# Keeping five of sixteen weight pieces of a feed-forward layer in SBUF in a fused RWKV block

## The chip, the cores and the metric

The kernel runs on one core of a Trainium2 chip. The metric is the device time of one launch in microseconds. The core has five engines that run their own instruction streams and wait for each other through semaphores: TensorE (PE), VectorE (DVE), ScalarE (ACT), GpSimd (POOL) and SyncE (SP), whose queue issues nearly all transfers here. Sixteen DMA engines move the data.

## The reference

x has shape (4, 2048, 512), fp32, 8192 tokens. The attention half works on a layer norm of x; the feed-forward half on a layer norm of what comes out.

```python
xx = jnp.pad(x, ((0, 0), (1, 0), (0, 0)))[:, :T] - x
r, k, v, g = (x + xx * maa_m) @ Wm.T ...        # 512 x 512 each, 32 heads of 16
# in chunks of 64 tokens, with a state per head:
att = rc @ kc * w_mat
yc = att @ vc + rc @ state * wb
state = ws * state + kc * wk @ vc
x = x + (group_norm(y) * silu(g)) @ Wo.T
# feed-forward, 512 -> 2048 -> 512
D = gelu(layernorm(x).astype(float16) @ W0.T + bias0).astype(float16)
x = x + (D @ W1.T + bias1).astype(float16)
```

## The kernel before

The tokens go through in nb = 32 blocks of 256 (two tiles of 128). A step n does the attention of block n, the rest of the attention (group norm, gate, output projection Wo) of block n-1, the feed-forward of block n-2 up to the first half of its down projection, and the second half of the down projection of block n-3. The order of the work on each engine is written out by hand (pe_step, dve_steady, act_steady, sp_steady); every dependence is a semaphore with a constant count. Steps 3 to 31 are alike ("steady"); there x and y are transposed by DMA (x_words, y_words) and not on TensorE.

The feed-forward weights are 16 pieces of 0.5 MB: pieces 0 to 7 for the up projection (W0), 8 to 15 for the down projection (W1). Each piece is [128, 2048] fp16: a scaled high part and a low part that the fp16 rounding of the high part left. Steps 0 and 1 prepare them ("PREPARED_AT"): load raw fp32 (sp_raw), square sums on ScalarE (act_piece_square, L382), a scaled high half (act_high), its transpose by DMA (sp_high), the transposed low half through TensorE (pe_prepare L836, act_prepare L851), and two stores of both halves to the DRAM tensor wd (sp_prepared). place_of says where piece j is prepared: slots of ring for j < 5, then hT, then a half of x1.

From step 2 on all 16 pieces are streamed once per block from wd through ring, which has RING = 5 slots. Transfer number `use` goes into slot use % 5 and is issued by sp_weights as soon as the piece five uses before has been consumed (s_up or s_dn). TensorE waits for s_w of the slot in pe_up (16 matmuls of 256 columns per piece) and pe_down (8 of 512 columns per piece).

In a steady step TensorE does, in this order: K0, down 4, K1, down 5, R0, down 6, R1, down 7, V0, up 0, V1, up 1, up 2, up 3, scores, kv, G0, up 4, scores, up 5, G1, up 6, att·v, up 7, from_state, scores, Wo 0, down 0, kv, scores, down 1, Wo 1, down 2, att·v, from_state, down 3. The scores, kv, att·v and from_state parts are many short matmuls of 64 rows. K, R, V and G are projections at L879 and L911, Wo is L1040, up is L1068, down is L1132, scores L941, from_state L982, kv L1012.

SP's queue in a steady step (sp_steady) issues: weights for `use` 0 to 2, the transpose for the feed-forward input (sp_fx), kx, x_words, weights 3, rx, the kN transpose (L2027), weights 4, y_words (L2043), weights 5, vbd (L2051), weights 6, vbd, out, weights 7 to 9, x1's load of x (L2077), xa's load of x (L2080), weights 10 to 15. An SP instruction that waits holds up all that stand behind it.

Of the kernel before, what the change touches and what calls it, by code (L numbers as in the profile page):

```python
# [21 lines left out]
NH = HID // P  # L22
UNITS = 16
RING = 5
LN_EPS = 1e-5
GN_EPS = 1e-5 * 144
KS = 2.0 ** 10
# [65 lines left out]
def program(nc, ctx, a, consts, x, out, wd, nb):  # L93
# [26 lines left out]
    f_scl = sb("f_scl", [P, PIECES + 1])  # L120
    f_sum = sb("f_sum", [P, 2 * PIECES])
    f_most = sb("f_most", [P, 1])
    ring = sb("ring", [P, RING, 2, 2 * C], F16)
    hT = sb("hT", [P, NH, BT], F16)
    x1 = sb("x1", [P, 2, NT, C])
# [219 lines left out]

    def place_of(j):
# [7 lines left out]
    def raw_piece(j):  # L356
        return place_of(j).bitcast(F32)

    def parts_of(j):

        return place_of(j)[:, 0:2 * C], place_of(j)[:, 2 * C:4 * C]

    def sp_raw(eng, n, j):
        if n == 0:
            source = W0[2 * P * j:2 * P * (j + 1), :]
        else:
            eng.wait_ge(s_stash[j], 32)
            source = W1[:, 2 * P * j:2 * P * (j + 1)]
        if n == 0:
            eng.dma_start(raw_piece(j).rearrange("p (b c) -> p b c", b=2),  # L370
                          source.rearrange("(b p) c -> p b c", p=P)).then_inc(s_raw[j], 16)
        else:
            for i in range(2):
                eng.dma_start(raw_piece(j)[:, C * i:C * i + C].rearrange("p (b c) -> p b c", b=G),
                              source[:, P * i:P * i + P].rearrange("(b p) c -> p b c", p=P)).then_inc(s_raw[j], 16)

    def act_piece_square(eng, n, j, squares):
        q = PIECES * n + j
        eng.wait_ge(s_raw[j], 48 if n else 16)
        if due(q):  # L380
            eng.wait_ge(s_psq, q)
        eng.activation(squares, raw_piece(j), ACT.Square, accum_out=f_sum[:, q:q + 1]).then_inc(s_psq, 1)  # L382

    def dve_power(eng, k, done, at, most, root, scale):

# [415 lines left out]
    def act_high(eng, q):  # L801

        k = min(q, PIECES)
        eng.wait_ge(s_pscl, POW2_PER * (q // PIECES) + POW2_PER - 1)
        if q <= PIECES:
            if k >= DIAGONALS:
                eng.wait_ge(s_ptr, k - DIAGONALS + 1)
            eng.activation(diagonals[k % DIAGONALS], ident[:, :], ACT.Identity, scale=f_scl[:, k:k + 1]).then_inc(s_diag, 1)
        eng.wait_ge(s_raw[q % PIECES], 48 if q >= PIECES else 16)
        j = q % PIECES  # L810
        if j % 3 == 2:
            eng.wait_ge(s_vwl, NT * (q // PIECES + 1))
# [4 lines left out]
        eng.activation(high(q), raw_piece(q % PIECES), ACT.Identity, scale=f_scl[:, k:k + 1]).then_inc(s_phi, 1)  # L817

    def pe_prepare(eng, n, place):

        q = piece(n, place)
        if q is None:
            return
        k = min(q, PIECES)
        eng.wait_ge(s_raw[q % PIECES], 48 if q >= PIECES else 16)
        eng.wait_ge(s_minus, 1)
        eng.wait_ge(s_diag, k + 1)
        eng.wait_ge(s_phi, q + 1)
        if due(q):
            eng.wait_ge(s_plo, q)  # L830
        else:
            eng.wait_ge(s_wlo, 10)
        for i in range(2):
            for b in range(G):
                at = C * i + P * b
                eng.matmul(F[:, i, rows(b)], raw_piece(q % PIECES)[:, at:at + P], diagonals[k % DIAGONALS],  # L836
                           start=(b == 0), stop=False)
            for b in range(G):
                at = C * i + P * b
                mm = eng.matmul(F[:, i, rows(b)], high(q)[:, at:at + P], minus_one[:, :],  # L840
                                start=False, stop=(b == G - 1))
        mm.then_inc(s_ptr, 1)

    def act_prepare(eng, n, place):

        q = piece(n, place)
        if q is None:
            return
        eng.wait_ge(s_ptr, q + 1)
        eng.wait_ge(s_psq, q + 1)  # L850
        eng.activation(parts_of(q % PIECES)[1], F[:, :, :].rearrange("p k c -> p (k c)"), ACT.Copy).then_inc(s_plo, 1)  # L851
        if q == 1:
            act_high(eng, 2)
        if 0 < q < PIECES - 2 or PIECES <= q < 2 * PIECES - 2:
            act_high(eng, q + 2)

    def sp_high(eng, q):

        eng.wait_ge(s_ptr, q + 1)
        eng.wait_ge(s_psq, q + 1)  # L860
        eng.dma_start_transpose(parts_of(q % PIECES)[0].rearrange("p (k c) -> p k c", c=P), high(q)).then_inc(
            s_phT[q % PIECES], 16)

    def sp_prepared(eng, q):
        j = q % PIECES
        eng.wait_ge(s_plo, q + 1)
        eng.wait_ge(s_phT[j], 16 * (q // PIECES + 1))
        for a in range(2):
            eng.dma_start(wd[q].rearrange("p (k a c) -> p a k c", k=2, a=2)[:, a],
                          parts_of(j)[a].rearrange("p (k c) -> p k c", k=2)).then_inc(s_stash[j], 16)  # L870

# [176 lines left out]
    def pe_up(eng, n, j):  # L1048

        f = n - 2  # L1050
        use = UNITS * f + j
        eng.wait_ge(s_w[use % RING], 16 * (use // RING + 1))
        if j == 0:
            eng.wait_ge(s_fx, 16 * (f + 1))
        if j >= 2:
# [9 lines left out]
        for i in range(2):  # L1065
            for a in range(2):
                for kk in range(G):
                    mm = eng.matmul(up_place(f, j)[:, i * BT:(i + 1) * BT],  # L1068
                                    ring[:, use % RING, i, a * C + kk * P:a * C + (kk + 1) * P], xT[:, :, kk, :],
                                    start=(kk == 0 and a == 0), stop=(kk == G - 1 and a == 1))  # L1070
        mm.then_inc(s_up, 1)

# [7 lines left out]
    def pe_last_down(eng):  # L1080
# [2 lines left out]
        eng.wait_ge(s_h, NH * nb)  # L1083
        for t, at, width, count in LAST_PARTS:
            for j in range(4, 8):
                use = UNITS * f + 8 + j
# [10 lines left out]
    def pe_down_of_last(eng, j):  # L1097

        f = nb - 1
        use = UNITS * f + 8 + j  # L1100
# [15 lines left out]
    def pe_down(eng, f, j):  # L1116
        if f == nb - 1:
            pe_down_of_last(eng, j)
            return
        use = UNITS * f + 8 + j  # L1120
# [874 lines left out]

    def sp_weights(eng, use):

        if use >= UNITS * nb:
            return
        gone = use - RING  # L2000
        if gone >= 0:
            f, i = gone // UNITS, gone % UNITS
            if i < 8:
                eng.wait_ge(s_up, 8 * f + i + 1)
            else:
                eng.wait_ge(s_dn, 8 * f + i - 7)
        eng.dma_start(ring[:, use % RING, :, :], wd[use % UNITS].rearrange("p (k e) -> p k e", k=2)).then_inc(
            s_w[use % RING], 16)

    def sp_stack(eng, dst, src, which, landed):  # L2010
# [41 lines left out]

    def sp_steady(eng, n, ahead):

        use = UNITS * (n - 2) - 4 + RING - 1
        p = n - 1
        for i in range(3):
            sp_weights(eng, use + i)
# [18 lines left out]
        eng.dma_start(x1[:, p % 2, :, :], x_rows(x, p)).then_inc(s_xr[p % 2], 16)  # L2077
        if n + 2 < nb:
            eng.wait_ge(s_xw, 2 * (n + 2 - BY_DMA))
            eng.dma_start(xa[:, :, :], x_rows(x, n + 2)).then_inc(s_xa, 16)  # L2080
        for i in range(10, 16):
            sp_weights(eng, use + i)

    def sp_step(eng, n):
        att_n, tail, ff, ahead, late = in_step(n)
        if tail and y_by_dma(n - 1):
            sp_steady(eng, n, ahead)
            return
        use = UNITS * (n - 2) - 4 + RING - 1
        if n > nb and ff:  # L2090
            sp_fx(eng, n - 2)
        if late:
# [29 lines left out]
        if ff:  # L2122
            sp_weights(eng, use + 5)
# [5 lines left out]
        if ff:  # L2129
            sp_weights(eng, use + 6)  # L2130
        if tail:
            p = n - 1
            if due(p - 1):
# [4 lines left out]
        if ff:  # L2138
            sp_weights(eng, use + 7)
        if n + 2 < nb:  # L2140
            if n + 1 < BY_DMA:
                eng.wait_ge(s_X, NT * (n + 2))
# [12 lines left out]
            sp_raw(eng, 1, PIECES - 1)  # L2155
        if n == 1:
            for j in range(PIECES):
                eng.wait_ge(s_stash[j], 64)
                if j < RING:
                    sp_weights(eng, j)  # L2160
        if ff:
            for i in range(8, 16):
                sp_weights(eng, use + i)

    steps = range(nb + 3)
# [83 lines left out]
```

## Time and profile before

| | us |
|---|---|
| median of 3 runs | 2085.12 (2084.56 to 2085.14) |
| the profiled execution, its own time | 2075.69 |
| its span, first to last instruction | 2073.9 |
| TensorE busy | 2002.3 |
| VectorE busy | 1738.2 |
| ScalarE busy | 1293.5 |
| DMA, main queue | 77.2% of 16 engines' span |

The profile shows one execution. Its times are counted from the first instruction. "Idle before" a group is time in which its engine did nothing, with what released it; "issue" stands where the profile shows nothing that the engine waited for. SPq is the time an instruction of SP's queue took to issue. The granted clock is a share of full speed; 1.00 is 2.4 GHz and 0.50 is 1.2 GHz.

### The profile page before, as it was taken

To read this page: it belongs to the slowest core of one execution; us is meant where nothing else is said; L and a number is where in the kernel's file an instruction comes from. 1 tells how busy PE (TensorE), PEld (TensorE's weight loads), DVE (VectorE), ACT (ScalarE), POOL (GpSimd) and SP (SyncE) were. 2 spreads that over 40 slices of the span, in tenths; PEclk is the share of its full clock that TensorE was granted. 3 is DMA by queue.
4 is the path that set the end of the run, shared out by engine and by line. 5 is a ranking of instruction groups with operands and counts; after the bars stand their busy time and mean duration, and the time that the engine had idled before them with its cause. 6 is when DMAs were issued, how large, how long until landed. Compare 5 with 4: busy or idle time off the path is not lost.

```text
span 2073.9 us, 64752 instructions
## 1 busy us (share of the span) xinstructions
PE 2002.3 (97%) x27206; PEld 1423.9 (69%) x27206; DVE 1738.2 (84%) x3687; ACT 1293.5 (62%) x2081; POOL 317.5 (15%) x329
## 2 busy tenths in 40 slices
PE   5889999999999999999999999999999999999999
PEld 5777667667666767766766776676776667667666
DVE  7778889888888988888988888898888888888761
ACT  7876565676566666655657765666765656666452
POOL 1111111111111111111111111111111111111110
PEclk8999999999999999999999999999999999999999
DMA  6977677888777788777778877778887877887777
GB/s 214 220 199 237 177 236 216 248 239 233 200 233 220 236 241 241 213 226 227 230 231 245 248 203 225 234 215 247 250 231 202 231 220 230 250 238 203 216 249 250
DMA packets 428979, 471.97 MB, mean 228 GB/s; under 512 B 259600, under 2 KB 309392, under 8 KB 428688
## 3 DMA queue, kind: packets, MB, share of 16 engines
q1 hardware_dynamic: 427056, 467.64, 77.2%
q8 instruction: 216, 3.54, 0.7%
q14 instruction: 75, 0.61, 0.1%
q10 hardware_dynamic: 1632, 0.18, 0.1%
HBM read 316.21 MB, written 25.17 MB: 165 GB/s over the span
## 4 chain that ended last, share of the span: by engine, by line
PE 81%; DMA 4%; SPq 4%; DVE 3%; ACT 3%; issue 3%; POOL 0%; ACTq 0%; DVEq 0%
PE F L1132 20%; PE F L1068 17%; PE B L879 10%; PE B L1040 8%; PE sc L879 7%; PE YT L911 6%; PE YT L879 3%; PE YT L963 2%; DMA y<-ygT 2%; PE sc L941 2%; PE YT L982 2%; DMA ring<-w_dram 1%; SPq L2027 1%; PE YT L1012 1%; PE F L836 1%
## 5 line engine op out<-in xcount | busy, mean ns | idle before, releaser
L1132 PE MATMUL F<-ring,hT 128*128 128x512 f16 x1984 | 467.5, 379 | 0.0
L1068 PE MATMUL F<-xT,ring 128*128 128x256 f16 x3840 | 449.3, 273 | 5.1 <-ACT hT L1768 3.7
L1068 PEld LDWEIGHTS F<-xT,ring 128*128 128x128 f16 x3840 | 369.8, 98 | 64.9 <-issue 8.0
L1132 PEld LDWEIGHTS F<-ring,hT 128*128 128x128 f16 x1984 | 189.1, 98 | 197.9 <-issue 0.5
L879 PE MATMUL B<-mix,WT 128*128 128x256 f16 x2304 | 267.5, 273 | 0.4 <-DVE gT L1372 0.3
L1768 ACT ACTIVATE hT<-F,b,f_rho 128x256 f16<-128x256 f32 x480 | 243.5, 560 | 37.9 <-PE F L1068 37.9
L879 PEld LDWEIGHTS B<-mix,WT 128*128 128x128 f16 x2304 | 222.6, 98 | 33.8 <-DVE gT L1372 0.6
L276 DVE SCALAR_TENSOR_TENSOR mixf<-dx,maa,xnT 128x256 f32<-128x256 f32 x512 | 238.6, 526 | 0.1
L1725 ACT ACTIVATE Shl<-S 128x256 f16<-128x256 f32 x128 | 53.1, 415 | 263.7 <-PE YT L982 148.6
L1971 POOL TENSOR_TENSOR Shl<-S,Shl 128x256 f16<-128x256 f32 x128 | 89.2, 697 | 734.7 <-ACT Shl L1725 734.7
L1719 ACT ACTIVATE att<-att 128x512 f16<-128x512 f32 x256 | 147.5, 624 | 68.3 <-DVE att L1333 68.3
L336 DVE TENSOR_TENSOR mix<-mixf,mix 128x1024 f16<-128x1024 f32 x128 | 184.0, 1438 | 2.9 <-ACT mix L332 1.8
L1040 PE MATMUL B<-WT,yg 128*128 128x512 f16 x768 | 180.1, 385 | 4.2 <-issue 4.2
L879 PE MATMUL sc<-mix,WT 128*128 128x256 f16 x1536 | 179.3, 274 | 4.7 <-issue 2.6
L1339 DVE TENSOR_TENSOR att<-att 128x512 f16<-128x512 f32 x256 | 166.7, 692 | 16.4 <-ACT att L1719 16.3
L911 PE MATMUL YT<-WT,mix 128*128 128x512 f16 x768 | 176.0, 379 | 0.6 <-DVE f_rho L389 0.3
L1333 DVE TENSOR_TENSOR att<-sc,wmask 128x512 f32<-128x512 f32 x256 | 164.2, 683 | 13.5 <-PE sc L941 13.1
L879 PEld LDWEIGHTS sc<-mix,WT 128*128 128x128 f16 x1536 | 150.6, 98 | 35.7 <-issue 5.2
L1976 POOL TENSOR_TENSOR x<-e,x 128x512 f32<-128x512 f16 x62 | 70.7, 1161 | 577.7 <-DVE e L1412 577.7
L332 ACT ACTIVATE mix<-mixf 128x1024 f16<-128x1024 f32 x128 | 134.6, 1051 | 4.6 <-DVE mixf L276 4.2
L1040 PEld LDWEIGHTS B<-WT,yg 128*128 128x128 f16 x768 | 72.9, 99 | 91.5 <-issue 9.1
L1654 ACT ACTIVATE kT<-sc 128x512 f16<-128x512 f32 x64 | 38.1, 596 | 155.0 <-PE sc L879 155.0
(196 smaller groups left out, 2997.6 us busy)
## 6 DMA issues: line engine op xcount, KB each, us to landing
ring<-w_dram SPq DMA_DIRECT2D x512, 512.0 KB, 4.6
kx<-kT SPq DMA_DIRECT2D x96, 256.0 KB, 3.8
rx<-rT SPq DMA_DIRECT2D x96, 256.0 KB, 4.4
xa<-in_L_attn_x SPq DMA_DIRECT2D x32, 512.0 KB, 7.6
vbd<-vN SPq DMA_DIRECT2D x256, 64.0 KB, 3.1
x<-in_L_attn_x SPq DMA_DIRECT2D x32, 512.0 KB, 6.1
out<-x SPq DMA_DIRECT2D x31, 512.0 KB, 3.8
w_dram<-ring SPq DMA_DIRECT2D x20, 256.0 KB, 3.8
```

The lines of the kernel that those rows point to most:

```text
L276: last = eng.scalar_tensor_tensor(out=mixf[:, m % 2, g, :], in0=dx[:, g, :], scalar=maa[:, m, g:g + 1], in1=xnT[:, g, 1:BT + 1], op0=ALU.m ...
L332: eng.activation(mix[:, m % 2, 0, :, :], mixf[:, m % 2, :, :], ACT.Copy).then_inc(s_mh, 1)
L336: eng.tensor_tensor(mix[:, m % 2, 1, :, :], mixf[:, m % 2, :, :], mix[:, m % 2, 0, :, :], ALU.subtract).then_inc(s_ml, 1)
L879: mm = eng.matmul(out[:, gg * BT:(gg + 1) * BT], WT[:, w, a, kk, rows(g)], mix[:, m % 2, b, kk, :], start=(i == 0 and kk == 0), stop=(i == ...
L911: mm = eng.matmul(Y[:, t, :], mix[:, 0, a, kk, rows(t)], WT[:, V_, b, kk, :], start=(i == 0 and kk == 0), stop=(i == 2 and kk == G - 1))
L1040: mm = eng.matmul(B[:, :], yg[:, a, kk, rows(t)], WT[:, O_, b, kk, :], start=(i == 0 and kk == 0), stop=(i == 2 and kk == G - 1))
L1068: mm = eng.matmul(up_place(f, j)[:, i * BT:(i + 1) * BT], ring[:, use % RING, i, a * C + kk * P:a * C + (kk + 1) * P], xT[:, :, kk, :], st ...
L1132: mm = eng.matmul(F[:, t, :], hT[:, k, rows(t)], ring[:, use % RING, i, a * C:(a + 1) * C], start=(k == 0 and a == 0), stop=(k == NH - 1 a ...
L1333: eng.tensor_tensor(att32[:, x, :], sc[:, x, :], wmask[:, 8 * x:8 * x + 8, :].rearrange("p q i -> p (q i)"), ALU.mult).then_inc(s_am, 1)
L1339: eng.tensor_tensor(att[:, c % 2, 1, C * x:C * x + C], att32[:, x, :], att[:, c % 2, 0, C * x:C * x + C], ALU.subtract).then_inc(s_al, 1)
L1719: eng.activation(att[:, c % 2, 0, C * x:C * x + C], att32[:, x, :], ACT.Copy).then_inc(s_ah, 1)
L1768: eng.activation(hT[:, k, :], up_place(f, j)[:, i * BT:(i + 1) * BT], ACT.Gelu, bias=b0[:, k:k + 1], scale=f_rho[:, j:j + 1]).then_inc(s_h, 1)
```

## The change

A tensor kept of [128, 5, 2, 1024] fp16 (20 KB per partition) is added. Up pieces 0 to 4 are prepared in it and stay there for the whole run; their stores to wd fall away. TensorE reads them from kept in pe_up, in the layout in which they were prepared (all high parts, then all low parts). The ring serves the other eleven pieces (up 5 to 7, down 0 to 7), so a step issues 11 weight transfers instead of 16. In the queue of a steady step, the weight issues around vbd and the three behind out fall away; xa's load moves ahead of x1's load, and between them stands weights 5, which waits for up 5. A scratch area that the program sets aside for DMA is made smaller (1024 bytes).

```diff
+KEPT = 5
+STREAMED = UNITS - KEPT
...
+    kept = sb("kept", [P, KEPT, 2, 2 * C], F16)
...
+    def place_of(q):
+        j = q % PIECES
+        if q < KEPT:
+            return kept[:, q, :, :].rearrange("p a e -> p (a e)")
         if j < RING:
             return ring[:, j, :, :].rearrange("p k e -> p (k e)")
...
     def sp_raw(eng, n, j):
         if n == 0:
             source = W0[2 * P * j:2 * P * (j + 1), :]
         else:
-            eng.wait_ge(s_stash[j], 32)
+            if j >= KEPT:
+                eng.wait_ge(s_stash[j], 32)
...
     def sp_prepared(eng, q):
         j = q % PIECES
+        if q < KEPT:
+            return
...
     def pe_up(eng, n, j):
-        use = UNITS * f + j
-        eng.wait_ge(s_w[use % RING], 16 * (use // RING + 1))
+        use = STREAMED * f + j - KEPT
+        if j >= KEPT:
+            eng.wait_ge(s_w[use % RING], 16 * (use // RING + 1))
+        elif f == 0:
+            eng.wait_ge(s_phT[j], 16)
...
+                    w = kept[:, j, a, i * C+at:i * C + at + P] if j < KEPT else ring[:, use % RING, i, a * C + at:a * C + at + P]
...
     def sp_weights(eng, use):
-        if use >= UNITS * nb:
+        if use >= STREAMED * nb:
             return
         gone = use - RING
         if gone >= 0:
-            f, i = gone // UNITS, gone % UNITS
+            f, i = gone // STREAMED, gone % STREAMED + KEPT
...
     def sp_steady(eng, n, ahead):
-        use = UNITS * (n - 2) - 4 + RING - 1
+        use = STREAMED * (n - 2)
...
         sp_weights(eng, use + 4)
         sp_y_words(eng, p)
-        sp_weights(eng, use + 5)
         sp_vbd(eng, n, 0)
-        sp_weights(eng, use + 6)
         sp_vbd(eng, n, 1)
         eng.wait_ge(s_o, NT * (n - 2))
         eng.dma_start(x_rows(out, n - 3), x1[:, (n - 3) % 2, :, :]).then_inc(s_st, 16)
-        for i in range(7, 10):
-            sp_weights(eng, use + i)
-        eng.wait_ge(s_st, 16 * (p - 1))
-        eng.dma_start(x1[:, p % 2, :, :], x_rows(x, p)).then_inc(s_xr[p % 2], 16)
         if n + 2 < nb:
             eng.wait_ge(s_xw, 2 * (n + 2 - BY_DMA))
             eng.dma_start(xa[:, :, :], x_rows(x, n + 2)).then_inc(s_xa, 16)
-        for i in range(10, 16):
+        sp_weights(eng, use + 5)
+        eng.wait_ge(s_st, 16 * (p - 1))
+        eng.dma_start(x1[:, p % 2, :, :], x_rows(x, p)).then_inc(s_xr[p % 2], 16)
+        for i in range(6, STREAMED):
             sp_weights(eng, use + i)
```

## Rows read from the trace of the kernel before

**Rows 1.** The page: busy times, DMA queues, one DMA issue with its landing.

```profile
PE 2002.3 (97%) x27206; PEld 1423.9 (69%) x27206; DVE 1738.2 (84%) x3687; ACT 1293.5 (62%) x2081; POOL 317.5 (15%) x329
...
q1 hardware_dynamic: 427056, 467.64, 77.2%
q8 instruction: 216, 3.54, 0.7%
...
x<-in_L_attn_x SPq DMA_DIRECT2D x32, 512.0 KB, 6.1
```

**Rows 2.** The chain that ended last, over the span: start us, us, what.

```profile
209.30 4.38 PE B L1040 x12
...
250.13 5.24 PE F L1068 x48
...
271.05 2.70 PE B L1040 x12
...
310.19 5.24 PE F L1068 x48
...
1861.78 4.24 PE B L1040 x12
...
1962.52 5.24 PE F L1068 x48
```

**Rows 3.** Waits of TensorE from 250 to 2000: us in total, times, longest.

```profile
PE sc L941 <- issue: 12.3, 11, 2.5
PE YT L982 <- issue: 4.4, 4, 1.3
PE B L1040 <- issue: 4.2, 3, 2.3
PE F L1068 <- ACT hT L1768: 2.9, 6, 0.7
```

**Rows 4.** Timeline of TensorE, two of the gaps.

```profile
1249.65 0.32 PE L941 MATMUL sc<-rx,kx 64*64 64x64 f16 x15 [1.48 <-issue]
...
1682.36 0.28 PE L941 MATMUL sc<-rx,kx 64*64 64x64 f16 x9 [0.83 <-issue]
```

**Rows 5.** Windows: us, busy of each engine (instructions), PEclk, DMA share, GB/s.

```profile
1861.40:1864.90 3.50, 3.44 (x15) 1.38 (x16) 3.09 (x5) 1.69 (x3) 0.00 (x0) 0.51 0.82 325
1244.29:1248.29 4.00, 3.88 (x148) 3.19 (x145) 3.36 (x6) 3.56 (x8) 0.97 (x1) 1.00 1.03 392
1248.29:1252.29 4.00, 2.64 (x27) 1.30 (x28) 3.93 (x7) 2.45 (x6) 0.67 (x1) 1.00 1.04 416
...
1256.29:1264.29 8.00, 8.00 (x142) 4.34 (x141) 4.91 (x13) 2.00 (x4) 1.28 (x2) 1.00 0.48 169
```

**Rows 6.** Timeline of SP's queue in an undisturbed step: start us, us.

```profile
1162.64 4.18 SPq L2027 DMA_TRANSPOSE kN<-kT  x1
...
1179.06 2.54 SPq L2007 DMA_DIRECT2D ring<-w_dram  x3
1182.62 0.38 SPq L2077 DMA_DIRECT2D x<-in_L_attn_x  x1
```

**Rows 7.** Timeline of SP's queue in step 1.

```profile
115.18 2.78 SPq L2027 DMA_TRANSPOSE kN<-kT  x1
```

**Rows 8.** Waits from 84 to 125: us in total, times, longest.

```profile
PE B L343 <- ACT xa L284: 1.9, 1, 1.9
...
ACT ygT L382 <- DMA x<-in_L_ffn_W: 0.7, 1, 0.7
```

**Rows 9.** Waits of TensorE from 2000 to the end.

```profile
PE YT L1068 <- DMA ring<-w_dram: 1.0, 1, 1.0
```

**Rows 10.** Timeline of TensorE in the step of rows 6.

```profile
1178.17 1.92 PE L1068 MATMUL F<-xT,ring 128*128 128x256 f16 x16
...
1188.16 2.76 PE L1040 MATMUL B<-WT,yg 128*128 128x512 f16 x12
...
1195.12 2.75 PE L1040 MATMUL B<-WT,yg 128*128 128x512 f16 x12
```

More of the change, by code:

```diff
@@ L344, in pe_X @@
         tr.then_inc(s_X, 1)
-    def place_of(j):
+    def place_of(q):
+        j = q % PIECES
+        if q < KEPT:
+            return kept[:, q, :, :].rearrange("p a e -> p (a e)")
         if j < RING:
@@ L354, in place_of, with raw_piece, parts_of, stashed @@
         return x1[:, 1, :, :].rearrange("p t c -> p (t c)").bitcast(F16)
[L356 to L361, printed above, removed]
+    def raw_piece(q):
+        return place_of(q).bitcast(F32)
+    def parts_of(q):
+        return place_of(q)[:, 0:2 * C], place_of(q)[:, 2 * C:4 * C]
+    def stashed(j):
+        return 32 if j < KEPT else 64
     def sp_raw(eng, n, j):
@@ L366, in sp_raw @@
         else:
-            eng.wait_ge(s_stash[j], 32)
+            if j >= KEPT:
+                eng.wait_ge(s_stash[j], 32)
             source = W1[:, 2 * P * j:2 * P * (j + 1)]
         if n == 0:
-            eng.dma_start(raw_piece(j).rearrange("p (b c) -> p b c", b=2),
+            eng.dma_start(raw_piece(PIECES * n + j).rearrange("p (b c) -> p b c", b=2),
                           source.rearrange("(b p) c -> p b c", p=P)).then_inc(s_raw[j], 16)
@@ L373, in sp_raw @@
             for i in range(2):
-                eng.dma_start(raw_piece(j)[:, C * i:C * i + C].rearrange("p (b c) -> p b c", b=G),
+                eng.dma_start(raw_piece(PIECES * n + j)[:, C * i:C * i + C].rearrange("p (b c) -> p b c", b=G),
                               source[:, P * i:P * i + P].rearrange("(b p) c -> p b c", p=P)).then_inc(s_raw[j], 16)
@@ L381, in act_piece_square @@
             eng.wait_ge(s_psq, q)
-        eng.activation(squares, raw_piece(j), ACT.Square, accum_out=f_sum[:, q:q + 1]).then_inc(s_psq, 1)
+        eng.activation(squares, raw_piece(q), ACT.Square, accum_out=f_sum[:, q:q + 1]).then_inc(s_psq, 1)
     def dve_power(eng, k, done, at, most, root, scale):
@@ L816, in act_high @@
             eng.wait_ge(s_phT[(6, 7, 5)[j]], 16)
-        eng.activation(high(q), raw_piece(q % PIECES), ACT.Identity, scale=f_scl[:, k:k + 1]).then_inc(s_phi, 1)
+        eng.activation(high(q), raw_piece(q), ACT.Identity, scale=f_scl[:, k:k + 1]).then_inc(s_phi, 1)
     def pe_prepare(eng, n, place):
@@ L835, in pe_prepare @@
                 at = C * i + P * b
-                eng.matmul(F[:, i, rows(b)], raw_piece(q % PIECES)[:, at:at + P], diagonals[k % DIAGONALS],
+                eng.matmul(F[:, i, rows(b)], raw_piece(q)[:, at:at + P], diagonals[k % DIAGONALS],
                            start=(b == 0), stop=False)
@@ L850, in act_prepare @@
         eng.wait_ge(s_psq, q + 1)
-        eng.activation(parts_of(q % PIECES)[1], F[:, :, :].rearrange("p k c -> p (k c)"), ACT.Copy).then_inc(s_plo, 1)
+        eng.activation(parts_of(q)[1], F[:, :, :].rearrange("p k c -> p (k c)"), ACT.Copy).then_inc(s_plo, 1)
         if q == 1:
@@ L860, in sp_high @@
         eng.wait_ge(s_psq, q + 1)
-        eng.dma_start_transpose(parts_of(q % PIECES)[0].rearrange("p (k c) -> p k c", c=P), high(q)).then_inc(
+        eng.dma_start_transpose(parts_of(q)[0].rearrange("p (k c) -> p k c", c=P), high(q)).then_inc(
             s_phT[q % PIECES], 16)
@@ L869, in sp_prepared @@
             eng.dma_start(wd[q].rearrange("p (k a c) -> p a k c", k=2, a=2)[:, a],
-                          parts_of(j)[a].rearrange("p (k c) -> p k c", k=2)).then_inc(s_stash[j], 16)
+                          parts_of(q)[a].rearrange("p (k c) -> p k c", k=2)).then_inc(s_stash[j], 16)
     def pe_project_T(eng, out, w, n, m, half):
@@ L1067, in pe_up @@
                 for kk in range(G):
-                    mm = eng.matmul(up_place(f, j)[:, i * BT:(i + 1) * BT],
-                                    ring[:, use % RING, i, a * C + kk * P:a * C + (kk + 1) * P], xT[:, :, kk, :],
+                    at = kk * P
+                    w = kept[:, j, a, i * C + at:i * C + at + P] if j < KEPT else ring[:, use % RING, i, a * C + at:a * C + at + P]
+                    mm = eng.matmul(up_place(f, j)[:, i * BT:(i + 1) * BT], w, xT[:, :, kk, :],
                                     start=(kk == 0 and a == 0), stop=(kk == G - 1 and a == 1))
@@ L1085, in pe_last_down @@
             for j in range(4, 8):
-                use = UNITS * f + 8 + j
+                use = STREAMED * f + 8 - KEPT + j
                 if t == 0:
@@ L1099, in pe_down_of_last @@
         f = nb - 1
-        use = UNITS * f + 8 + j
+        use = STREAMED * f + 8 - KEPT + j
         eng.wait_ge(s_w[use % RING], 16 * (use // RING + 1))
@@ L1119, in pe_down @@
             return
-        use = UNITS * f + 8 + j
+        use = STREAMED * f + 8 - KEPT + j
         eng.wait_ge(s_w[use % RING], 16 * (use // RING + 1))
@@ L2006, in sp_weights @@
                 eng.wait_ge(s_dn, 8 * f + i - 7)
-        eng.dma_start(ring[:, use % RING, :, :], wd[use % UNITS].rearrange("p (k e) -> p k e", k=2)).then_inc(
+        eng.dma_start(ring[:, use % RING, :, :], wd[KEPT + use % STREAMED].rearrange("p (k e) -> p k e", k=2)).then_inc(
             s_w[use % RING], 16)
@@ L2088, in sp_step @@
             return
-        use = UNITS * (n - 2) - 4 + RING - 1
+        use = STREAMED * (n - 2)
         if n > nb and ff:
@@ L2121, in sp_step @@
                               x1[:, (n - 3) % 2, t, at:at + width]).then_inc(s_st, 16)
-        if ff:
-            sp_weights(eng, use + 5)
         if att_n:
@@ L2128, in sp_step @@
             sp_prepared(eng, PIECES * n)
-        if ff:
-            sp_weights(eng, use + 6)
         if tail:
@@ L2137, in sp_step @@
             eng.dma_start(x1[:, p % 2, :, :], x_rows(x, p)).then_inc(s_xr[p % 2], 16)
-        if ff:
-            sp_weights(eng, use + 7)
         if n + 2 < nb:
@@ L2157, in sp_step @@
             for j in range(PIECES):
-                eng.wait_ge(s_stash[j], 64)
+                eng.wait_ge(s_stash[j], stashed(j))
                 if j < RING:
@@ L2161, in sp_step @@
         if ff:
-            for i in range(8, 16):
+            for i in range(5, STREAMED):
                 sp_weights(eng, use + i)
@@ L2231 @@
     from concourse.bass_utils import run_bass_kernel_spmd
-    nc = bacc.Bacc("TRN2", target_bir_lowering=False, num_devices=1)
+    nc = bacc.Bacc("TRN2", target_bir_lowering=False, num_devices=1, dynamic_dma_scratch_size=1024)
     arrays, aps, consts = {}, {}, {}
```

## The prediction, made before the changed kernel was run

> **What bounds the kernel now.** I read the page's busy shares first: TensorE is busy 97% of the span, VectorE 84%, ScalarE 62%, and the 16 DMA engines 77% [rows 1]. So only a little time can come back at all, and it has to come back on TensorE. I then measured what a step costs when nothing disturbs it. The same matmul group of the up projection starts at 250.13 and at 310.19: 60.06 us. From 250.13 to 1962.52 there are 28 steps, so a mean step is 61.16 us [rows 2]. The steady part therefore holds 28 x 1.10 = 30.8 us above its floor; the head holds some idle time more and the tail very little.
>
> The waits of TensorE between 250 and 2000 say what the excess is [rows 3]: 18 gaps, 12.3 + 4.4 + 4.2 = 20.9 us, in which the engine waited for nothing that the profile shows ("issue"), and 2.9 us for ScalarE's GELU. Not one microsecond is put down to a weight transfer. A kernel that looks as if it had a stream of 0.5 MB weights to get rid of is not waiting for weights.
>
> Where do the 18 gaps lie? I went through the timeline of TensorE. 14 of them, all of those above 0.9 us, lie in the short matmuls (64x64) behind up piece 7 of a step or in the first output projection right after; one of 1.48 us is shown. The other four, 0.83 us and less, come in the short matmuls behind down piece 0 [rows 4]. In the two windows that hold the gap of 1.48 us the DMA engines' share is 1.03 and 1.04. In the 8 us from 1256.29, with more short matmuls (x142 in all), the share is 0.48 and TensorE has no gap [rows 5]. The page has a queue that explains such gaps: "q8 instruction", 216 packets, 3.54 MB [rows 1]. TensorE runs 27,206 matmuls and as many weight loads; 3.54 MB over 54,412 is 65 B each, so q8 is TensorE's own program, some 250 instructions to a packet. That is my inference: short matmuls use up instructions faster than the next packet comes, and the packet travels over the same DMA engines as everything else.
>
> **The change part by part.** *Transfers.* Each step issues 11 weight transfers instead of 16. The five that go from the SP queue of a step are one ahead of each of the two vbd groups and the three at 1179.06 [rows 6]; they are released by up 0 to up 4. What is issued between 1178 and 1192 today is out, three weights, x, xa and three more weights (for up 5, 6, 7): nine transfers of 0.5 MB. At the 416 GB/s of the full window [rows 5] one takes 1.26 us, nine 11.3 us of 14: full, as the share says. After the change the same stretch has out, xa, x and three weights, six of them, 7.6 us; out and xa come 1 to 2 us earlier, since every removed issue ahead of them held SP (0.85 us each in the group of three). The share there should fall from 1.0 to about 0.5 to 0.6.
>
> *What this is worth in the 18 gaps.* The trace shows no packet's latency, so I bound it: nothing, if the time from request to use doesn't depend on the load, and all 20.9 us, if it does strongly. The nearest row is another operation that goes through the same engines: the kN transpose holds SP for 4.18 us in a loaded step and for 2.78 us in step 1, where fewer transfers are in flight [rows 6, 7], 1.4 us less. Gaps of 1.16 us mean that lose 1.4 us each would nearly vanish. Since the load halves and doesn't go away, I take two thirds: 14 us.
>
> The Trainium skill speaks against this ("Runtime: NRT & Kernel Launch", Instruction fetch mechanics): TensorE has a FIFO for 2048 instructions, refilled in blocks of 256, and crossing a block is "mostly hidden". The block agrees with 3.54 MB in 216 packets; "hidden" doesn't agree with the 20.9 us of issue gaps, unless these have another cause. By the rule the term would be 0 instead of 14 us, and the whole sum 8 us instead of 22.
>
> *What follows a gap.* Of the 30.8 us, about 20 are the issue gaps and 2.9 the GELU's; some 7.8 us are left. 1.5 us of that is a stretch right after the longest gap, in which the granted clock is 0.51, the lower of the two levels (1.2 GHz), and twelve matmuls take 4.24 us instead of 2.70 [rows 2, 5]. The rest are slivers around the gaps. They should go with their cause: I take 4 us, bounds 0 and 7.8.
>
> *The head.* Ten stores of 256 KB to DRAM go (pieces 0 to 4, two each), and the second half's loads of pieces 0 to 4 no longer wait for them. SP is the late one there: ScalarE waits 0.7 us for the last load of the second half, and TensorE, behind ScalarE, 1.9 us for the normalised xa [rows 8]. Of these about 1 us should go. At 209 us a gap is followed by twelve matmuls in 4.38 us instead of 2.70 [rows 2]; a part of gap and slow clock I count too, 2 us. That makes 3 us for the head; the bounds are 0 and 6 (1.9, 1.7 for the clock, and a gap of at most 2.5).
>
> *The tail.* Here a weight does stop TensorE, once, for 1.0 us at an up piece [rows 9]. Five of each block's up pieces need no load any more, so the ring runs further ahead. I take 1.3 us with the slivers beside it, bounds 0 and 2.
>
> *Costed at nothing.* Reading kept instead of ring costs TensorE the same matmul. Five waits per step are taken from it. The steady steps' 2.9 us of waits for the GELU come from the chain kx, x_words, rx, kN, y_words in SP's queue; all five weight issues ahead of y_words stay (same slots, same releases), so I take 0, bound 2.9. The other order: x1's load now stands behind the weights that wait for up 5. Up 5 ends at 1180.09 and x is issued at 1182.62 today [rows 6, 10]; it will come no later. xa moves ahead and is needed only in the next step. Weights 6 to 10 wait for up 6 and later, as their counterparts do today, and each is used over 10 us later.
>
> *Sum.* 14 + 4 + 3 + 1.3 = 22.3 us of the profiled execution's 2075.7 us (span 2073.9), which gives 2053.4 us. The shown median, 2085.1 us, is 9.4 us above that execution, and the trace can't say why. I take the same 22 us from it: 2063 us.
>
> **The rivals.** (a) *The gaps don't depend on the DMA load.* Then the tail's 1.3 us, the 1 us of the late load and some of the GELU waits remain: about 3.5 us, 2081.6 us, inside what counts as no change. For it: the gaps share the place of the shortest matmuls as well as that of the fullest DMA, and a single packet needs little bandwidth. Against: the second group of short matmuls has none. The Trainium skill's page "DMA: Bandwidth & Descriptors" (Queues, rings and completion order) has each DMA engine take turns between queues packet by packet, by which a full weight queue would delay a packet of the program hardly at all; no row shows the order, and by that rule this case holds.
>
> (b) *The gaps go entirely,* with the slivers, the clock and the GELU waits: 20.9 + 7.8 + 6 + 2 + 2.9 = 39.6 us, 2045.5 us. For it: the removed transfers stand right ahead of the gaps. Against: w for up 6 and up 7 still land in the middle of that stretch.
>
> (c) *Slower: the load of x comes late.* Place: the residual add behind the first output projection (L1303), which reads x1; the second projection waits for it. x is issued at 1182.62, lands 6.1 us later at 1188.7, the projection ends at 1190.9, and the second starts at 1195.1 [rows 1, 6, 10]. With 0.7 us for the add, the load may come 5.6 us later than now before TensorE stands. Each microsecond beyond is paid in 29 steps; if it came 6 us later, 0.4 x 29 = 12 us, 2075 us with the other gains, and at 7 us late 1.4 x 29 = 41 us, 2104 us. Against: the only new thing ahead of it is the wait for up 5, 2.5 us before its issue now.
>
> (d) *The stream shifts.* Five instructions fewer a step put the packet boundaries elsewhere. The boundaries already wander over the step (gaps come in only some steps), so I expect the same mean; if the shift were unlucky, a third more, 7 us, would come against a gain of 8: about 2084 us.
>
> **How the numbers follow.** Forecast 0.62; (a) 0.20; (b) 0.07; (c) 0.04; (d) 0.07. The forecast's own range is 2052 to 2075 us (gap term 7 to 20 us, slivers 1 to 7, head and tail 2 to 6). 0.2% of 2085 us, about 4 us, is what a measurement of this kernel can tell. The range 2050 to 2084 us takes in (a) and leaves out most of (b), (c) and half of (d). Faster: all of the forecast and (b), a quarter of (a), together 0.74. Same: the rest of (a) and half of (d), 0.18. Slower: (c) and half of (d), 0.08.
>
> **What would show it.** The DMA share over the span falls from 77% to about 67% (160 transfers of 1.26 us are 202 us, a tenth of the span), and in the 8 us behind up 6 of a step from 1.0 to about 0.6. "Issue" in TensorE's waits between 250 and 2000 falls from 20.9 to about 7 us and the mean step from 61.16 to below 60.6, the undisturbed step staying at 60.06. The tail shows no wait for ring. The GELU waits stay near 3 us. The prediction is wrong if the share falls and the issue gaps stay (a), or if L1303 waits for DMA (c).

## The result and the profile after

Five pieces kept took 31 us off. The changed kernel has a median of 2053.7 us (2050.8 to 2055.1, 4 runs) against 2084.8 us (2078.8 to 2085.1, 4 runs) for the kernel before; the ratio is 0.9855, 95% interval 0.9834 to 0.9877. Timed twice more it came to 0.9834 (0.9809 to 0.9859) and 0.9855 (0.984 to 0.987). The forecast was 2063 us, range 2050 to 2084: right in sign and mechanism, and 22 us where 31 were measured.

The page of the changed kernel, lines that answer to [rows 1]:

```profile
PE 1999.8 (98%) x27206; PEld 1424.3 (70%) x27206; DVE 1738.7 (85%) x3687; ACT 1293.0 (63%) x2081; POOL 317.5 (15%) x329
...
q1 hardware_dynamic: 401296, 381.12, 68.1%
q8 instruction: 215, 3.52, 0.7%
...
x<-in_L_attn_x SPq DMA_DIRECT2D x32, 512.0 KB, 5.0
```

TensorE does the same work (2.5 us less of busy time), the data queue carries 86.5 MB less and its share falls from 77.2% to 68.1%, as forecast (about 67%). q8, read in the prediction as TensorE's own program, has 215 packets instead of 216: if program delivery improved, it isn't because there is less of it. (With the five waits a step put back, e1 below, it is 216 again.)

The chain that ended last, same points as [rows 2]:

```profile
250.53 5.24 PE F L1086 x48
...
310.65 5.24 PE F L1086 x48
...
1940.54 5.24 PE F L1086 x48
```

The span falls by 24.9 us (2073.9 to 2049.0), and the three rows divide it. The head up to the first row is 0.4 us longer. The 28 steps between first and last row take 1690.0 instead of 1712.4 us, 22.4 less: 60.36 us a step instead of 61.16, over a floor of 60.1 that has not moved (250.53 to 310.65). The tail behind the last row is 108.5 instead of 111.4 us, 2.9 less.

Waits of TensorE in the steady part (248 to 1975 us), against [rows 3]:

```profile
PE F L1086 <- ACT hT L1785: 4.1, 8, 0.7
PE YT L995 <- issue: 0.5, 1, 0.5
PE F L1149 <- issue: 0.5, 1, 0.5
```

The issue gaps fell from 20.9 us in 18 places to 1.0 us in two (3.5 us in five places and 3.4 us in four in two more executions of the changed kernel). One of the 18, 1.1 us, lay behind 1962.52 and so counts for the tail; within the 28 steps it is 19.9 against 1.0 us, 18.9 less. The waits for the GELU went from 2.9 to 4.1 us. That makes 17.7 of the 22.4 us; the other 4.7 are what the prediction called slivers (idle pieces beside the gaps) and the slow clock behind them.

What the DMA engines do around the short matmuls has to be read at one offset in the step. The offset is counted from the start of the step's first value projection (V, L911 before, L924 after, 12 matmuls of 128x512). The two windows of full share in [rows 5] lie 24 to 28 and 28 to 32 us behind such a start (1220.29), around the short matmuls where most of the gaps lay. The same offsets in one step of the changed kernel (columns as in rows 5):

```profile
1172.47:1176.47 4.00, 4.00 (x163) 3.35 (x161) 2.80 (x6) 3.02 (x7) 0.47 (x1) 1.00 0.52 177
1176.47:1180.47 4.00, 4.00 (x27) 1.87 (x20) 3.93 (x7) 2.45 (x6) 0.67 (x1) 1.00 0.46 135
```

The share there was 1.03 and 1.04; now it is 0.52 and 0.46, while TensorE is busy for all of the 4 us of each window. Over all 29 steady steps the two windows have a mean share of 1.01 and 0.99 in the kernel before and of 0.67 and 0.42 in the changed one. The engines are no longer full, though far from idle.

### The profile page after: what moved, and what is told of

The parts are those of the page before. It is cut to its first block, busy times and chain, and to the rows that moved or that the text cites. A ratio compares the mean times of both kernels' runs of the same rounds, so it can differ in the third digit from the quotient of the medians.

```text
span 2049.0 us, 64453 instructions
## 1 busy us (share of the span) xinstructions
PE 1999.8 (98%) x27206; PEld 1424.3 (70%) x27206; DVE 1738.7 (85%) x3687; ACT 1293.0 (63%) x2081; POOL 317.5 (15%) x329
## 3 DMA queue, kind: packets, MB, share of 16 engines
q1 hardware_dynamic: 401296, 381.12, 68.1%
## 4 chain that ended last, share of the span: by engine, by line
PE 81%; SPq 4%; DVE 4%; ACT 4%; DMA 3%; issue 2%; POOL 0%; ACTq 0%; DVEq 0%
PE F L1149 19%; PE F L1086 16%; PE B L892 9%; PE B L1053 8%; PE sc L892 7%; PE YT L924 6%; PE YT L892 3%; DMA y<-ygT 3%; PE YT L976 3%; SPq L2044 2%; PE sc L954 2%; PE YT L995 2%; PE YT L1086 1%; PE F L847 1%; PE YT L1025 1%
## 5 line engine op out<-in xcount | busy, mean ns | idle before, releaser
L1086 PE MATMUL F<-xT,kept 128*128 128x256 f16 x2400 | 276.8, 273 | 2.0 <-issue 1.2
L1086 PEld LDWEIGHTS F<-xT,kept 128*128 128x128 f16 x2400 | 234.6, 98 | 42.1 <-issue 2.6
L924 PE MATMUL YT<-WT,mix 128*128 128x512 f16 x768 | 178.6, 383 | 1.3 <-DVE mix L339 0.9
L1086 PE MATMUL F<-xT,ring 128*128 128x256 f16 x1440 | 172.5, 273 | 4.1 <-ACT hT L1785 4.1
L1086 PEld LDWEIGHTS F<-xT,ring 128*128 128x128 f16 x1440 | 135.3, 98 | 23.3 <-issue 6.4
```

Of the source, the lines that this page charges most:

```text
L924: mm = eng.matmul(Y[:, t, :], mix[:, 0, a, kk, rows(t)], WT[:, V_, b, kk, :], start=(i == 0 and kk == 0), stop=(i == 2 and kk == G - 1))
L1086: mm = eng.matmul(up_place(f, j)[:, i * BT:(i + 1) * BT], w, xT[:, :, kk, :], start=(kk == 0 and a == 0), stop=(kk == G - 1 and a == 1))
```

## The experiments

The result leaves open whether the bytes, the place of the transfers, the order in the queue, the removed waits or the shifted instruction stream did it. Each ratio is to the kernel before on the same chip: 2081.1 us beside e1 to e4, 2083.8 us beside e5 to e7, 2081.7 us beside e8 and the last comparison. "Steady issue gaps" are TensorE's, summed over its waits from about 248 to 1975 us; the kernel before has 19.9 us of them.

**e1_waits_back: the stream.** The changed kernel with the five TensorE waits of a block put back, in each block, on a semaphore that has long been reached:

```
-        elif f == 0:
+        else:
             eng.wait_ge(s_phT[j], 16)
```

> The changed kernel, with one thing put back: in every block TensorE waits once more at each of up 0 to up 4, on a semaphore that is long past its value, so that its instruction stream is as long as in the kernel before, while the eleven transfers stay. Theory 1 (the issue gaps come from the DMA load ahead of them): no difference to the changed kernel, about 2051 to 2055 us, issue gaps between 250 and 1975 of 1 to 3 us. Rival (the shorter stream moved the packet boundaries of TensorE's program off the short matmuls): the gaps come back, 15 us or more of issue, 2070 us or more.

Measured: 2049.2 us, ratio 0.9859 (0.9835 to 0.9883), steady issue gaps 1.2 us. The gain stays, so neither the removed waits nor the shift of the instruction stream made it.

**e2_scratch_only: the SBUF that made room.** The kernel before with nothing but the smaller descriptor scratch that the change also sets:

```
-    nc = bacc.Bacc("TRN2", target_bir_lowering=False, num_devices=1)
+    nc = bacc.Bacc("TRN2", target_bir_lowering=False, num_devices=1, dynamic_dma_scratch_size=1024)
```

> The kernel before with the smaller scratch area for DMA and nothing else. Theory 1: nothing changes, a ratio of 1.000 within 0.2%, issue gaps near 21 us. Rival (the scratch size itself is part of the gain): a ratio below 0.996.

Measured: 2082.6 us, ratio 1.0019 (1.0005 to 1.0033), steady issue gaps 23.7 us. It gives nothing. It also serves as a second look at the kernel before: its profiled execution (2082.3 us) lies at the median of the kernel before, where the one of [rows 1] (2075.7 us) lies 9 us under it.

**e3_again_same_place: the bytes back, where they were.** The changed kernel, in which the five kept pieces are stored to DRAM in the head and read again into kept in every step: one ahead of each vbd group and three behind out, the places of the five transfers that the change removed. The part of the edit in SP's queue for a steady step:

```
+        sp_again(eng, n - 2, 0)
         sp_vbd(eng, n, 0)
+        sp_again(eng, n - 2, 1)
         sp_vbd(eng, n, 1)
         eng.wait_ge(s_o, NT * (n - 2))
         eng.dma_start(x_rows(out, n - 3), x1[:, (n - 3) % 2, :, :]).then_inc(s_st, 16)
+        for j in range(2, KEPT):
+            sp_again(eng, n - 2, j)
```

> The changed kernel, but the five kept pieces are stored to DRAM after all and loaded again into kept once per block, each as soon as its up piece is done, at the places in SP's queue where the five transfers stood before (one ahead of each vbd group, three behind out). TensorE's loads of its program and its matmuls are as in the kernel before, the transfers are sixteen again. Theory 1: the issue gaps come back, 15 to 21 us between 250 and 2000, and the time goes to 2072 to 2085 us. Rival (kept as such or the shorter stream or the order of xa and x was what helped): it stays within 5 us of the changed kernel, 2050 to 2058 us.

**e4_again_late: the same bytes, later.** As e3, but all five reads stand last in the step, behind the weights that wait for down 2:

```
         for i in range(6, STREAMED):
             sp_weights(eng, use + i)
+        for j in range(KEPT):
+            sp_again(eng, n - 2, j)
```

> The same sixteen transfers per block as in the run that loads kept again at the old place, but the five are issued at the end of the step, behind the weights that wait for down 2, where the DMA engines are half idle. Theory 1 (what counts is the backlog on the DMA engines just ahead of the short matmuls, not the bytes): issue gaps of 1 to 4 us, 2052 to 2060 us. Rival (the bytes per step count, wherever they are moved): gaps of 15 us or more and 2072 us or more, as at the old place.

Measured: e3 2078.8 us, ratio 0.9991 (0.9973 to 1.001); e4 2063.2 us, ratio 0.9927 (0.9904 to 0.9951), above the 2052 to 2060 us expected of it. In e3 the whole gain is gone. Its waits of TensorE, 248 to 1975 us:

```profile
PE sc L956 <- issue: 12.3, 10, 2.5
PE B L1055 <- issue: 4.7, 3, 2.0
PE F L1090 <- ACT hT L1789: 4.3, 9, 0.7
PE YT L997 <- issue: 3.4, 4, 1.1
```

The issue gaps are back at 20.4 us, on the lines and in the sizes of the kernel before. The same waits in e4:

```profile
PE F L1090 <- ACT hT L1789: 3.0, 8, 0.7
PE sc L956 <- issue: 0.9, 1, 0.9
```

The data queue moved 465.02 MB in either, at 77.1% in e3 and 77.5% in e4, and they have 20.4 and 0.9 us of issue gaps. The bytes don't decide. The windows 24 to 28 and 28 to 32 us behind a V start, e3 first:

```profile
1557.54:1561.54 4.00, 4.00 (x153) 3.36 (x151) 3.46 (x7) 3.69 (x7) 1.25 (x2) 1.00 1.01 389
1561.54:1565.54 4.00, 2.25 (x30) 1.07 (x21) 3.93 (x7) 2.38 (x5) 0.67 (x1) 1.00 1.04 410
```

and the same step of e4, with the window 44 to 52 us behind the start as third:

```profile
1534.68:1538.68 4.00, 3.89 (x152) 3.22 (x149) 3.38 (x6) 3.60 (x8) 0.97 (x1) 1.00 0.76 264
1538.68:1542.68 4.00, 3.98 (x29) 1.94 (x30) 3.93 (x7) 2.45 (x6) 0.67 (x1) 1.00 0.42 138
...
1554.68:1562.68 8.00, 8.00 (x61) 5.63 (x59) 7.55 (x27) 2.39 (x5) 0.00 (x0) 1.00 0.95 380
```

In e3 the engines are full and TensorE stands for 1.75 of 4 us. In e4 the load is moved to a stretch of large matmuls, where the share is 0.95, and TensorE does not stop there. So nearly full DMA engines cost TensorE nothing under its large matmuls; they cost where its short ones come.

e4's steady step is that of the changed kernel: its x48 groups start at 251.12 and 1940.14, 60.32 us a step. The 14 us by which its median stays behind e1's on the same chip must lie elsewhere. Behind the last x48 row it takes 123.1 us (changed kernel: 108.5), and the timeline of TensorE there has most of the difference:

```profile
1988.61 5.97 PE L1090 MATMUL YT<-xT,kept 128*128 128x256 f16 x32 [5.72 <-issue]
...
2029.22 7.02 PE L1090 MATMUL YT<-xT,kept 128*128 128x256 f16 x40 [4.29 <-issue]
```

These are up 0 of the last two blocks, in steps without an attention part, 10 us together. Ahead of each, SP's queue:

```profile
1974.34 1.17 SPq L2036 DMA_DIRECT2D kept<-w_dram  x2
...
1978.98 3.85 SPq L2062 DMA_TRANSPOSE xT<-xh  x1
...
2016.69 2.69 SPq L2036 DMA_DIRECT2D kept<-w_dram  x5
2019.47 4.13 SPq L2062 DMA_TRANSPOSE xT<-xh  x1
```

The reloads are issued right ahead of the xT transpose, and up 0 needs both. So these two gaps, though named "issue", look like late data of the experiment's own making; e8 tests that.

**e5_old_order: the order of x and xa.** The changed kernel with the old order of the two loads:

```
+        eng.wait_ge(s_st, 16 * (p - 1))
+        eng.dma_start(x1[:, p % 2, :, :], x_rows(x, p)).then_inc(s_xr[p % 2], 16)
         if n + 2 < nb:
...
-        sp_weights(eng, use + 5)
-        eng.wait_ge(s_st, 16 * (p - 1))
-        eng.dma_start(x1[:, p % 2, :, :], x_rows(x, p)).then_inc(s_xr[p % 2], 16)
-        for i in range(6, STREAMED):
+        for i in range(5, STREAMED):
```

> The changed kernel with the old order of the two loads of x in a steady step: x1's load behind the out store, then xa's, then all weights from 5 on. Eleven transfers. Theory 1 (backlog): six transfers stand in that stretch either way, so gaps of 0 to 4 us and the time within 3 us of the changed kernel on the same chip. Rival (moving xa ahead was a part of the gain): 5 us or more above it.

Measured: 2055.3 us, ratio 0.9856 (0.9833 to 0.9879), steady issue gaps 7.2 us; the changed kernel beside it 2051.1 us, 0.9834, gaps 3.5 us. The expectation, gaps of 0 to 4 us and a time within 3 us, was missed on both counts. The old order costs some 4 us, with intervals that overlap: by the medians, an eighth of the gain lies in the order. What it does to the DMA engines is clear: x1's load waits there until out has landed, xa's load stands behind it, and both come later and closer to the short matmuls (in one step x is issued 21.1 and xa 21.5 us behind the V start, in the changed kernel 20.3 and 17.5). The mean share in the window 24 to 28 us behind the V start is 0.91 instead of 0.67.

**e6_weights_behind_y: fewer transfers ahead of the y transpose.** The changed kernel with weights 3 and 4 of a step moved behind y_words, one ahead of each vbd:

```
-        sp_weights(eng, use + 3)
         sp_rx(eng, n)
         sp_k_tokens(eng, n)
-        sp_weights(eng, use + 4)
         sp_y_words(eng, p)
+        sp_weights(eng, use + 3)
         sp_vbd(eng, n, 0)
+        sp_weights(eng, use + 4)
         sp_vbd(eng, n, 1)
```

> The changed kernel with weights 3 and 4 of each steady step issued behind y_words (one ahead of each vbd group) instead of ahead of rx and of y_words. What is left of the steady excess in the changed kernel is TensorE's wait for the GELU, 4.1 us in 8 gaps, and slivers around it. Theory 1: the y_words transpose is late because SP's queue and the DMA engines are full ahead of it, so y_words lands 2 to 4 us earlier, the waits for the GELU nearly vanish, the mean step goes from 60.36 to 60.1 us, and the kernel is 4 to 8 us faster than the changed one. Rival (ScalarE's own work sets that wait, or the two transfers now collide with vbd or refill the stretch ahead of the short matmuls): no gain, or gaps of issue come back.

Measured: 2047.2 us, ratio 0.9813 (0.9793 to 0.9833). Its waits of TensorE, 248 to 1975 us:

```profile
PE sc L954 <- issue: 1.6, 2, 1.0
PE F L1149 <- issue: 0.7, 2, 0.4
```

and its chain:

```profile
249.92 5.24 PE F L1086 x48
...
1935.44 5.24 PE F L1086 x48
```

There is no GELU wait left, and the step is 60.20 us. The chain kx, x_words, rx, kN, y_words that the prediction named is shortened by it; SP's queue of the changed kernel and then of e6:

```profile
1150.45 4.29 SPq L2044 DMA_TRANSPOSE kN<-kT  x1
1154.78 1.05 SPq L2024 DMA_DIRECT2D ring<-w_dram  x1
1155.88 3.36 SPq L2060 DMA_TRANSPOSE y<-ygT  x1
```

```profile
1147.39 2.89 SPq L2044 DMA_TRANSPOSE kN<-kT  x1
1150.33 3.06 SPq L2060 DMA_TRANSPOSE y<-ygT  x1
```

Counted from the V start (1148.47 and 1145.64), the y transpose is issued at 4.7 instead of 7.4 us. kN holds SP for 2.89 instead of 4.29 us when no weight was issued just ahead of rx and kN; over the 29 steady steps the medians are 2.9 and 4.2 us.

**e7_kept2: a smaller dose.** KEPT = 2, so 14 transfers a step.

```
-KEPT = 5
+KEPT = 2
```

> The changed kernel with KEPT = 2, so fourteen transfers a step instead of eleven; two of the five are gone. Theory 1 (the backlog just ahead of the short matmuls, 1.26 us for a transfer, sets the gaps): the backlog shrinks by 2.5 us instead of 6.3 us. If the gaps end only when the backlog has drained before the program's packet is asked for, most of the 21 us stay (10 us or more); if they shrink with each transfer, about 8 to 12 us are left. Total 2062 to 2075 us. Rival (any kept piece is enough): gaps below 4 us and 2050 to 2056 us.

Measured: 2072.9 us, ratio 0.9948 (0.9929 to 0.9966), steady issue gaps 16.6 us. Two fifths of the transfers give a third of the gain (0.52% of 1.66%). Of the gap time they give between a sixth and a third: 16.6 us against 19.9 us in the kernel before and 23.7 us in e2. The first window is as full as before (mean share 1.01 over the 29 steps), only the second begins to empty (0.86). That fits a gain that hangs on how far the backlog has drained when the short matmuls come. One execution of e7, beside a spread of 19.9 to 23.7 us at its upper end, can't tell a steep fall from a proportional one.

**e8_late_steady: e4 without the reloads in its tail.** Reloads stop before the last two blocks, which read the kept pieces as they lie:

```
-        if f + 1 >= nb:
+        if f + 3 >= nb:
             return
...
-            eng.wait_ge(s_raw[j], 48 + 16 * f)
+            eng.wait_ge(s_raw[j], 48 + 16 * min(f, nb - 3))
```

> This is the kernel e4_again_late (all sixteen pieces moved in every step, the five reloads of the kept pieces last in the step) with one difference: the reloads stop before the last two blocks, whose steps are short, so that the last two blocks use the kept pieces as they lie. 153 of the 155 kinds of load per piece stay: 29 blocks' worth of five reloads against 31. Theory backlog (the gain comes from the place at which the DMA engines are full, not from the bytes; the 12 us that e4 lay above the changed kernel were two waits of up 0 for late reloads in the last two blocks): the two gaps at 1988 and 2029 us go, the span falls from 2063 to about 2052, ratio to the kernel before near 0.986, TensorE issue gaps in the steady stretch stay near 1 us, queue 1 near 460 MB and 77%. Rival, bytes: the extra traffic itself costs what e4 showed above the changed kernel (spread over the run, not in the tail): the span stays near 2063 and the ratio near 0.993.

Measured: 2051.4 us, ratio 0.9858 (0.9841 to 0.9874). 145 reloads are left of e4's 155 (the expectation has the count wrong). The gap of 5.72 us has become one of 0.46 us, that of 4.29 us is gone, and steady issue gaps are 1.9 us. So the two gaps of e4 were late data of its own reloads. Its data queue, on the page:

```profile
q1 hardware_dynamic: 423616, 459.78, 77.5%
```

A kernel that moves 79 MB more than the changed one takes the same time to 0.03%, with intervals of 0.16% (changed kernel 0.9855, below).

**e6_again and after_third.** The faster order once more beside the changed kernel, no edit.

> e6_weights_behind_y once more beside a run of the changed kernel on the same chip. If its 4 us below the changed kernel are real (the GELU waits of 3 to 4 us gone because the transfers that compete with them are later), the ratio is near 0.982 and that of the changed kernel near 0.984; if they were scatter between programs, both come out within 0.1% of one another.

> The changed kernel again, for comparison with e8_late_steady and e6_again on the same chip: near 0.984 to 0.986.

Measured: e6 2046.0 us, 0.9835 (0.982 to 0.985); the changed kernel 2049.9 us, 0.9855 (0.984 to 0.987). In both comparisons e6 is 3.9 us below it. Either pair of intervals overlaps, the two together speak for a real 0.2%.

**All runs side by side.** The mean DMA share of the two windows over the 29 steady steps, and the steady issue gaps:

| | 24 to 28 us | 28 to 32 us | issue gaps, us |
|---|---|---|---|
| kernel before | 1.01 | 0.99 | 19.9 |
| e2 | 1.00 | 0.99 | 23.7 |
| e3 | 0.99 | 1.00 | 20.4 |
| e7 | 1.01 | 0.86 | 16.6 |
| e5 | 0.91 | 0.46 | 7.2 |
| e1 | 0.69 | 0.44 | 1.2 |
| e8 | 0.67 | 0.43 | 1.9 |
| changed kernel, three executions | 0.65 to 0.67 | 0.41 to 0.42 | 1.0, 3.5, 3.4 |
| e4 | 0.66 | 0.43 | 0.9 |
| e6 | 0.48 | 0.41 | 2.3 |

The gaps fall all the way from full engines to a share of about a half, and e5 lies in between; below that there is little left to gain.

**Whether TensorE waits for its program.** The traces hold the start and the length of each packet of q8, and they settle what the prediction could only infer. Count TensorE's instructions (matmuls, weight loads and waits) in order of their start. The steady issue gaps of the thirteen traces are 102. Every one of them ends at an instruction whose number leaves 193, 194 or 195 when divided by 256, and 1.0 to 1.6 us after a packet of q8 has landed. The packets have 16,384 bytes each, and the kernel before has 55,257 such instructions for its 216 packets, 256 to a packet. So a gap is TensorE standing at the end of a block of 256 instructions until the next one is there (the record begins inside a block, so the remainder isn't 0). Most crossings don't show: the kernel before has 186 in the steady part, 17 of them with a gap.

The packet itself isn't slower on full engines, it starts later. The six runs below have the same number of TensorE instructions, so a block holds the same work in each. Means over the 17 blocks that end in a gap in the kernel before, in us:

| | packet starts, after the block's start | packet takes | block takes, with its gap |
|---|---|---|---|
| kernel before | 3.2 | 1.0 | 5.6 |
| e2 | 3.3 | 1.0 | 5.7 |
| e3 | 3.0 | 1.0 | 5.6 |
| e1 | 0.9 | 1.2 | 4.3 |
| e4 | 1.2 | 1.1 | 4.3 |
| e8 | 1.0 | 1.1 | 4.4 |

A block of short matmuls can be over in 3.2 us. With the packet starting 3.2 us after the block, taking 1.0 and being of use some 1.4 us later, the next block can't begin before 5.6 us; with a start at 1.0 us it can after 3.5 us, and hardly a gap is left. Blocks of large matmuls take up to 18.9 us. In e4 the packets of blocks over 7.5 us start later than in the changed kernel (1.2 against 0.6 us on average), and it doesn't matter there.

## Why the prediction was right, and where it was too small

**Steady gap term: 14 us forecast, 18.9 us measured** (and 1.1 in the tail) between the two profiled executions; 16.4 and 16.5 with the other two executions of the changed kernel. The mechanism held: the share falls, the gaps fall, the bytes put back in place (e3) bring both back, and put elsewhere (e4, e8) bring neither; and the inference that q8 is TensorE's program and that its packets come late is borne out by the traces. The step that was mis-sized is "since the load halves and doesn't go away, I take two thirds". A load that halves (0.67 and 0.42 in the two windows) leaves no third of the gaps but 1.0 to 3.5 us: the packet needn't be as early as on idle engines, only early enough for a block of 256 instructions. The working on the way there has a slip: nine transfers in 11.3 of 14 us are a share of 0.8 and not "full, as the share says"; the rest was other traffic. Of rival (b) the gap term came true, the GELU term didn't.

**Slivers and clock behind gaps: 4 us forecast,** 4.7 measured.

**Head: 3 us forecast, none found.** The gap and the slow clock at 209 us went, worth 3.5 us where 2 were forecast, but up to the first row of the chain the changed kernel is 0.4 us longer. It loses the time in the preparation: a group of 24 matmuls that starts at 141.14 us before starts at 145.05 us. TensorE still waits 2.2 us there for the normalised xa (1.9 before, [rows 8]), and 1.8 us for ScalarE at one piece. The 1 us expected from the earlier loads is not to be seen. The first row comes at 247.7 to 250.5 us in three executions of the changed kernel and at 249.4 us in e2, so these differences are within what executions differ by. No experiment took the head apart.

**Tail: 1.3 us forecast, 2.9 measured.** The wait for ring [rows 9] is gone, as said. The rest is mostly the issue gap of 1.1 us behind the last row of the chain.

**GELU waits: forecast to stay near 3 us, measured 4.1** (3.2 and 2.3 in two more executions). Costing it at nothing was right, and e6 shows that the reason given was right too: with two weights taken out of that chain the waits are zero.

**The gap to the median.** The terms summed to 22.3 us, the profiled pair gives 24.9 us (10% off), the timed medians give 31. That the sum came so close is in part luck: a head 3.4 us too high stands against a gap term 4.9 us too low. The remainder is the choice of executions: the sum was made against one of 2075.7 us where the median was 2085.1, and the changed kernel's profiled one (2050.8 us) lies only 2.9 us under its median. The prediction said that the trace couldn't say why. e2, whose profiled execution lies at that median, can: its 28 steps (249.42 to 1968.59) take 1719.2 us, 6.8 more than [rows 2] and 29.2 more than the changed kernel's; its issue gaps there are 23.7 us instead of 19.9, and what is neither gap nor GELU wait above 28 floors of 60.06 us is 11.0 us, against 7.9 in the execution before and 3.2 after. So an ordinary execution of the kernel before seems to hold more gap and more sliver than the one profiled, and both go with the change; e2 stands in for it, since it differs by the scratch alone. To subtract 22 us from the median was to price the change on an execution with less of the trouble.

**The rivals.** (a), gaps independent of load, is refuted by e3 against e4. The Trainium skill ("Runtime: NRT & Kernel Launch", Instruction fetch mechanics) says that crossing a block of the program is mostly hidden. By count that holds here, 169 of 186 crossings show no gap; but it can't be read as a term of 0, since the 17 others held 19.9 us. The Trainium skill's page "DMA: Bandwidth & Descriptors" (Queues, rings and completion order) has the DMA engines take turns between queues; the prediction's reading of it, that a full weight queue would then delay a program packet hardly at all, is not borne out: its start moves by some 2 us. (c), x too late: x is issued 20.3 us behind the V start instead of 22.4, lands in 5.0 instead of 6.1 us, and no wait of VectorE in the steady part names a DMA. (d), the stream shift, is refuted by e1.

**What stays open.** Why a packet of the program starts 2 us later when the engines are full, though it takes no longer itself: the traces show its start, not when it was asked for or what it stood behind. It wasn't tried to give the same short matmuls other neighbours at a full DMA, nor to move transfers in the kernel before, whose ring needs pieces 5 to 7 in that very stretch.

## What to carry to other kernels

"Issue" gaps in bursts of short matmuls can be a DMA cost although no wait names a DMA: look at the DMA share in the few microseconds around them, not at the share over the span, and at when the packets of the program start and land. Transfers need not go, they need to be elsewhere: e8 has the whole gain at a share of 77.5%, though it took places of their own in SBUF to make those five free to move. And price a change on an execution at the median; on one that happened to run 9 us faster, the fault that you remove is smaller than it is.

## What the runs showed of the hardware that was not expected

- TensorE's issue gaps come at the end of a block of 256 instructions, 1.0 to 1.6 us behind the landing of a 16,384 byte packet of q8 (102 gaps in thirteen traces). With full DMA engines that packet starts some 2 us later (3.0 to 3.3 against 0.9 to 1.2 us after the block's start) and takes no longer.
- The gaps were 19.9 to 23.7 us where both windows around the short matmuls had a mean share of 0.99 to 1.01, 16.6 us at 1.01 and 0.86, 7.2 us at 0.91 and 0.46, and 0.9 to 3.5 us at 0.48 to 0.69 and 0.41 to 0.44.
- A share of 0.95 at 380 GB/s under large matmuls cost TensorE nothing (e4, 28 steps of 60.32 us).
- The kN transpose held SP for 2.9 us in the median step of e6 and for 4.2 us in that of the changed kernel, which issues a weight of 0.5 MB ahead of it.
- The smaller descriptor scratch alone came out 0.19% slower (0.05 to 0.33%) in its one comparison, no more than what the prediction took as the limit of such a measurement.
